# Seven block products instead of eight for the last batch's queries and keys, in a fused attention and FFN kernel

## The reference

```
q  = ln(x) @ W_q.T ;  kv = ln(x) @ W_kv.T           # 16 heads of 32
qf = fft(q) per head, divided by its norm ;  kvf likewise
kvf = cumsum(kvf over the rows of the batch)
x  = x + ifft(qf * kvf).real @ W_o.T
g  = silu((ln(x) @ fp8(gate_w)) * gate_scale) ;  u = (ln(x) @ fp8(up_w)) * up_scale
x  = x + ((g * u) @ fp8(down_w)) * down_scale       # inner width 1536
```

## Time and profile before

| what | value |
|---|---|
| time, median of 3 runs | 422.57 us (422.27 to 423.33) |
| profiled execution, span from first to last instruction | 419.2 us (the profile gives no other time for it) |
| TensorE busy | 411.5 us, 98% |
| VectorE busy | 281.3 us, 67% |
| ScalarE busy | 193.4 us, 46% |
| GpSimd busy | 102.5 us, 24% |
| granted TensorE clock, mean | 0.998 |

### The profile page before, as it was taken

One profiled execution on the slowest core, in us unless ns is written; L12 is line 12 of the kernel. 1 busy time (PEld: TensorE's weight loads), 2 busy tenths in 40 slices (PEclk: granted clock), 3 DMA queues, 4 the chain that ended last, 5 costly groups with the idle time before them and its releaser, 6 DMA issues.

```text
span 419.2 us, 5474 instructions
## 1 busy us (share of the span) xinstructions
PE 411.5 (98%) x1895; PEld 218.8 (52%) x1895; DVE 281.3 (67%) x497; ACT 193.4 (46%) x322; POOL 102.5 (24%) x108
## 2 busy tenths in 40 slices
PE   8999999999999999999999999999999999999994
PEld 4744454455455554554554564454555555555553
DVE  5999998999999694287676952186784744332234
ACT  3787656676755245546222573255342522122220
POOL 0133641015334322045350031043541001300003
PEclk9999999999999999999999999999999999999999
DMA  8986548600381144140112025320112041200002
GB/s 249 289 240 238 177 101 187 141 2 0 94 209 26 38 64 88 39 167 34 27 33 44 2 50 89 62 95 7 25 27 52 0 90 37 75 2 0 2 0 100
DMA packets 57546, 33.54 MB, mean 80 GB/s; under 512 B 49456, under 2 KB 49840, under 8 KB 57392
## 3 DMA queue, kind: packets, MB, share of 16 engines
q1 hardware_dynamic: 57088, 32.93, 30.7%
q10 hardware_dynamic: 432, 0.28, 0.2%
HBM read 17.44 MB, written 4.19 MB: 52 GB/s over the span
## 4 chain that ended last, share of the span: by engine, by line
PE 95%; DMA 1%; DVE 1%; SPq 1%; POOL 0%; POOLq 0%; issue 0%
PE bd L461 21%; PE bu L445 20%; PE bg L445 20%; PE ba L350 15%; PE ba L390 8%; PE bd L350 4%; PE ba L363 1%; DMA h<-x_dram 1%; PE bd L390 1%; PE bd L363 1%; PE bg L350 1%; PE bu L350 1%; PE bu L390 1%; PE bd L407 1%; PE bd L336 0%; PE bg L422 0%
## 5 line engine op out<-in xcount | busy, mean ns | idle before, releaser
L461 PE MATMUL bd<-dw,fu 128*128 128x512 f32 x376 | 100.0, 411 | 0.0
L445 PE MATMUL bu<-hT,gu 128*128 128x512 f16 x384 | 90.7, 379 | 0.0
L445 PE MATMUL bg<-hT,gu 128*128 128x512 f16 x376 | 89.2, 380 | 0.0
L461 PEld LDWEIGHTS bd<-dw,fu 128*128 128x128 f32 x376 | 70.6, 188 | 18.6 <-DVE fu L1165 0.7
L1160 DVE SCALAR_TENSOR_TENSOR ff<-bu,us,sl 128x512 f32<-128x512 f32 x48 | 35.9, 747 | 65.0 <-PE bu L445 61.8
L708 ACT ACTIVATE sl<-bg,gs 128x512 f32<-128x512 f32 x48 | 32.9, 686 | 80.2 <-PE bg L445 79.3
L350 PE MATMUL ba<-wf,xT 128*128 128x512 f16 x288 | 63.2, 379 | 0.0
L445 PEld LDWEIGHTS bu<-hT,gu 128*128 128x128 f16 x384 | 37.4, 98 | 45.6 <-DVE ff L1160 0.6
L445 PEld LDWEIGHTS bg<-hT,gu 128*128 128x128 f16 x376 | 34.1, 98 | 45.8 <-issue 8.9
L1165 DVE TENSOR_TENSOR fu<-ff,fu 128x512 fp32r<-128x512 f32 x47 | 40.1, 856 | 15.7 <-ACT fu L714 15.3
L1534 POOL TENSOR_TENSOR h<-ff,h 128x512 f32<-128x512 f32 x14 | 17.6, 1277 | 129.8 <-DVE ff L1186 129.8
(11 more groups left out here) (180 smaller groups left out, 449.9 us busy)
## 6 DMA issues: line engine op xcount, KB each, us to landing
h<-x_dram SPq DMA_DIRECT2D x16, 256.0 KB, 4.2
out_dram<-h SPq DMA_DIRECT2D x15, 256.0 KB, 2.0
hT<-w_q_dram SPq DMA_DIRECT2D x4, 256.0 KB, 3.8
gu<-w_kv_dram SPq DMA_DIRECT2D x4, 256.0 KB, 4.7
hT<-gate_w_dram SPq DMA_DIRECT2D x2, 512.0 KB, 3.8
hT<-up_w_dram SPq DMA_DIRECT2D x2, 512.0 KB, 5.9
gu<-woT_dram SPq DMA_DIRECT2D x1, 1024.0 KB, 5.5
hT<-down_w_dram SPq DMA_DIRECT2D x2, 512.0 KB, 5.0
```

The costliest lines, as they stand in the source:

```text
L445: m = e.matmul(bk[:, :], gu[:, c, 4 * w + k, col:col + P], hT[:, b % 2, part, k, :], start=k == 0 and part == 0, stop=k == KT - 1 and part ...
L461: m = e.matmul(bd[t][:, :], fu_at(n)[:, part, P * t:P * t + P], dw[:, i, :], start=i == 0 and part == 0, stop=i == NI - 1 and part == 1)
```

## The change

The rows of batch 3 are taken as two halves (tiles 0 and 1, tiles 2 and 3), the inner dimension as two halves (slices 0 and 1, slices 2 and 3) and the weights as queries and keys. The two by two blocks are multiplied with seven products instead of eight (Strassen's algorithm in Winograd's form). One product of one row pair j is 2 slices times 3 parts = 6 matmuls, 14 products in all.

- The four sums of weights (`dve_t`, 16 operations, in f32) are made on VectorE in batch 1's pass and split in high (`act_th`, 8) and low parts (`dve_tl`, 8).
- The rows of batch 3 are normalised pair by pair (`dve_x7`) and four sums of halves of them made (`dve_s7`, 256 columns each). Seven blocks of 256 columns per pair are rounded, split (`act_xh7`, `pool_xl7`) and transposed (`sp_x7`), where `xT` had four of 128 per tile.
- The products are added up in PSUM and by VectorE (`dve_u2`, `dve_u3`, `dve_c`, 10 operations); ScalarE copies two (`act_p1`, `act_first7`) and squares from SBUF (`act_sq7`). All 14 products stand ahead of batch 2's first gate/up step; none is left between the first two.
- The row statistics of batch 3 (`dve_stats1`, `dve_root0_head` and `_tail`) and its norm chain come earlier in VectorE's program. The constant that sets the scale of the folded weights is 2^-13 instead of 2^-14.

```diff
 tensor_program, pass b:
-                if nxt < NB:
+                if nxt < NB - 1:
                     pe_qk(e, nxt, 0, 0)
...
+                elif nxt < NB:
+                    for j in range(2):
+                        for p in SEVEN:                    # 1, 6, 2, 7, 5, 4, 3
+                            pe_seven(e, j, p)
                 pe_gate_up(e, b, 0)
                 pe_down(e, b * NI - 1)
-                if nxt < NB:
+                if nxt < NB - 1:
                     pe_qk(e, nxt, 3, 1)
 scalar_program, pass b:
                     act_qk(e, nxt, 1, 0)
+                    act_th(e, 0, 1)
                     act_qk(e, nxt, 1, 1)
+                    act_th(e, 0, 3)
                     act_qk(e, nxt, 2, 0)
+                    act_th(e, 0, 2)
+                    act_th(e, 0, 4)
+                    act_th(e, 1, 1)
+                    act_th(e, 1, 3)
+                    act_th(e, 1, 2)
+                elif nxt < NB:
+                    for j in range(2):
+                        act_p1(e, j)
+                        act_first7(e, j)
+                        act_sq7(e, j, 0)
...
                 act_silu(e, b * NI)
...
                 act_silu(e, b * NI + 3)
+                if b + 2 < NB:
+                    act_th(e, 1, 4)
 vector_program, pass b:
-                if nxt < NB:
+                if nxt < NB - 1:
                     dve_sum(e, nxt, 0, 0)
+                    dve_t(e, 0, 1)
                     dve_sum(e, nxt, 0, 1)
+                    dve_t(e, 0, 2)
+                    dve_t(e, 0, 3)
                     dve_sum(e, nxt, 1, 0)
+                    dve_t(e, 0, 4)
+                    dve_t(e, 0, 5)
                     dve_sum(e, nxt, 1, 1)
+                    dve_t(e, 0, 6)
+                    dve_t(e, 0, 7)
                     dve_sum(e, nxt, 2, 0)
+                    dve_t(e, 0, 8)
+                    dve_tl(e, 0, 1)
+                    dve_t(e, 1, 1)
+                    dve_tl(e, 0, 3)
+                    dve_t(e, 1, 2)
+                    dve_t(e, 1, 3)
+                    dve_tl(e, 0, 2)
+                    dve_t(e, 1, 4)
+                    dve_t(e, 1, 5)
+                    dve_t(e, 1, 6)
+                elif nxt < NB:
+                    for j in range(2):
+                        dve_u2(e, j)
+                        dve_u3(e, j)
+                        dve_sum(e, nxt, j, 0)
+                        dve_c(e, j, 5)
+                        dve_c(e, j, 4)
...
                 dve_scale_out(e, b - 1, 3)
-                if nxt < NB:
+                if nxt < NB - 1:
                     dve_sum(e, nxt, 3, 1)
+                elif nxt < NB:
+                    dve_norm_tail(e, nxt, range(NT))
+                    dve_scale(e, nxt, 0, 1)
                 dve_f(e, b * NI + 1)
...
                 dve_fu(e, b * NI + 1)
+                if b + 2 < NB:
+                    dve_tl(e, 0, 4)
+                    dve_t(e, 1, 7)
...
                     dve_product(e, nxt, 0)
+                if b + 2 < NB:
+                    dve_t(e, 1, 8)
+                    dve_tl(e, 1, 1)
+                    dve_tl(e, 1, 3)
                 dve_f(e, b * NI + 3)
...
                 dve_fu(e, b * NI + 3)
+                if b + 2 < NB:
+                    dve_tl(e, 1, 2)
+                    dve_tl(e, 1, 4)
+                    dve_stats1(e, b + 2, 1)
+                    dve_stats1(e, b + 2, 2)
                 if nxt < NB:
                     dve_zl(e, nxt, 1)
...
                     dve_o(e, nxt, 1)
+                if b + 2 < NB:
+                    dve_root0_tail(e, b + 2, range(NT))
+                    dve_x7(e, 0, 0)
+                    dve_x7(e, 0, 1)
+                    for n in (1, 2, 3, 4):
+                        dve_s7(e, 0, n)
```

More of the change, by code:

```diff
@@ L66, in tenancies @@
     for b in range(1, NB):
-        if b > 1:
-            order += [("qk", b, 0, w) for w in range(2)]
-        order += [("qk", b, t, w) for t in (1, 2, 3) for w in range(2)]
+        if b == NB - 1:
+            order += [("seven", j, p) for j in range(2) for p in SEVEN]
+        else:
+            if b > 1:
+                order += [("qk", b, 0, w) for w in range(2)]
+            order += [("qk", b, t, w) for t in (1, 2, 3) for w in range(2)]
         order += [("tri", b, 0)]
@@ L183, in build @@
         a_zh, v_zl = sem("act_zh"), sem("dve_zl")
+        s_seven, a_p1, a_xh7, p_xl7, a_th, v_tl = (
+            sem(n) for n in ("pe_seven", "act_p1", "act_xh7", "pool_xl7", "act_th", "dve_tl"))
+        v_t, v_x7, v_s7, v_u2, v_u3, v_c = (sem("dve_" + n) for n in ("t", "x7", "s7", "u2", "u3", "c"))
+        d_x7 = [sem(f"d_x7{n}") for n in range(3)]
         d_cst, d_cst2, d_id, d_wo, d_sc, d_carry = (sem("d_" + n) for n in ("cst", "cst2", "id", "wo", "sc", "carry"))
@@ L352, in pe_qk @@
             m.then_inc(s_qk, 1)
+        def pe_seven(e, j, p):
+            i, n = AT["seven", j, p], 7 * j + SEVEN.index(p)
+            held = {1: wf[:, 0, :, 0:2, :], 2: wf[:, 0, :, 2:4, :], 3: wf[:, 1, :, 2:4, :], 4: w_sum[4],
+                    5: w_sum[1], 6: w_sum[2], 7: w_sum[3]}[p]
+            vacant(e, ("seven", j, p))
+            e.wait_ge(d_x7[X_PIECE[p]], 32 * (j + 1))
+            if n == 1:
+                e.wait_ge(v_tl, 8)
+            first = p not in (2, 3)
+            for k in range(2):
+                for part_x, part_w in ((0, 0), (0, 1), (1, 0)):
+                    m = e.matmul(ba[i][:, :], xts[:, part_x, X_BLOCK[p] + k, P * j:P * j + P], held[:, part_w, k, :],
+                                 start=first and k == 0 and part_x == part_w, stop=k == 1 and part_x == 1,
+                                 skip_group_check=True)
+            m.then_inc(s_seven, 1)
         def pe_tri(e, b, t):
@@ L947, in scalar_program @@
                 act_silu(e, b * NI + 7)
+                if b + 2 < NB:
+                    act_root0(e, b + 2, range(NT))
+                    act_xh7(e, 0, 0)
+                    act_xh7(e, 0, 1)
+                    act_xh7(e, 0, 2)
                 if nxt < NB:
@@ L1587, in gpsimd_program @@
                 if b + 2 < NB:
[L1588 to L1591, removed]
+                    for j in range(2):
+                        for n in range(3):
+                            pool_xl7(e, j, n)
             pool_out(e, NB - 1, 0)
@@ L1606, in sp_xT, with sp_x7 @@
                 e.dma_start(xT[:, b % 2, part, :, P * t:P * t + P], xs[:, t % 2, part, :], transpose=True).then_inc(d_xT[t], 16)
+        def sp_x7(e, j, n):
+            lo, hi = X_COLS[n]
+            if j == 0 and n == 0:
+                e.wait_ge(s_qk, 8 * (NB - 1))
+            for part in range(2):
+                e.wait_ge((a_xh7, p_xl7)[part], 3 * j + n + 1)
+                e.dma_start(xts[:, part, lo // P:hi // P, P * j:P * j + P], xs7[:, part, lo:hi],
+                            transpose=True).then_inc(d_x7[n], 16)
         def sp_hT(e, b, t):
```

211 lines of the change are left out of this document (169 added, 42 removed).

## The result

The changed kernel takes 427.52 us (median of 6 runs, 426.48 to 429.62), the kernel before 422.42 in the same comparison (6 runs): ratio 1.0129, interval 1.0110 to 1.0148. It is 5.1 us slower. I had forecast 424.0 and a range to 426.3; slower was right, the size was not, and the time lies outside the range.

A forecast was written before the change was run, and what follows sets the result against it. TensorE was taken to bound the kernel, busy 411.47 of 419.20 us. The terms -2.60 + 1.15 + 1.6 + 0.6 + 0.1 + 0.6 = +1.45 us gave 424.0 us, range 420.9 to 426.3.

The forecast's parts named there:

- The saving: Twelve matmuls between batch 2's first two gate/up steps go: 2.60 us gained, the most the change can give.
- Step A: Start of batch 1's stretch: weight sums delay ScalarE's table load and first SiLU, TensorE waits for a bank; +1.15 us.
- Step B: Scan of batch 2: added VectorE operations and contention with GpSimd make tile 1's scan late; +1.6 us, bounds 0.3 to 3.5.
- Step C: Additions before zl(1): GpSimd's low part of ks for tile 3 late for its scan matmul; +0.6 us, bounds 0 to 1.2.
- The products of batch 3: The seven products per row pair run without stalls: 0 us, bounds 0 and 1.3.
- The transposes: 56 blocks instead of 32, 17.4 us of queue instead of 9.9, issued before they are needed: hidden.
- the rest of batch 1: Statistics and normalisations leave VectorE's queue later, where it is busy 11.67 of 18.00 us; +0.1 us, bounds 0 and 0.5.
- lower end of the sum: Saving with the lowest stalls: -2.60 + 0.3 + 0.3 = -2.0 us.
- Step D: FFN's start in batch 2: norm chain and a scale ahead of the second FFN product make it late; +0.6 us, 0.2 to 1.2.
- Rival 3: VectorE always goes first over GpSimd at the shared memory access, lengthening the scan's stalls: 426.4 us, chance 0.11.
- the first three: Rivals: additions absorbed, 421.1 us, chance 0.22; saving and stalls cancel, 422.4, 0.28; VectorE always first, 426.4, 0.11.
- rival 4: Matmul count stays or accumulating into a bank already read costs an interruption, no gain: about 426.6 us, chance 0.02.

The follow-up runs named there:

- run 5: Changed kernel with five late weight-sum operations moved from the scan of tiles 0 and 1 to behind the second attention output; 428.24 us, run once.
- run 1: Kernel before with only the 32 operations on weight sums added at the changed kernel's places, results unused; 426.16 us, ratio 1.0098.
- Run 3: Changed kernel with GpSimd's first low part of row pair 0 held back until VectorE's four half sums are done; 425.45 us, ratio 1.0078.
- no_sums: Changed kernel without the 32 weight-sum instructions, plain weight slices used in their place; 422.65 us, ratio 1.0014.
- late_sums2: late_sums with the norm chain between batch 2's scaled outputs and late fu parts ahead of the rows' normalisations; 420.97 us, ratio 0.9964 to the kernel before.
- Run 2: The same run as no_sums: changed kernel without the 32 weight-sum instructions; 422.65 us, 4.9 less than the changed kernel.
- late_sums: Changed kernel with roundings behind the first SiLU, GpSimd held back, norm chain behind the FFN product, seven weight-sum operations and pair 0's rows later; 422.38 us, ratio 1.0001.

## Why the prediction was wrong

**What held.** The bound was right: TensorE, where a late operand costs its lateness. The saving was 2.60 and nothing else shortened. Step A was right in its mechanism, and its wait by the bracket, 1.32 us, is 0.17 above the estimate (1.49 by the ledger, with the slower matmuls behind it); the last weight sum ended at 176.20 for 175.8 computed (the pass began 0.32 later). Step B was sized at 1.6 and is 1.85; its two parts, 0.85 by order and the rest by GpSimd, were found by run 5 as about 0.7 and 1.1. Step C was 0.6 and is 0.83, within its bounds, but not by the path that I named. The scan of tile 3 waits for nothing. The up step ahead of it waits 0.31 us: GpSimd's product of tile 1 ended late (two halves of 1.18 instead of 0.73, beside the low parts), and behind it ScalarE's copy, VectorE's `dve_zl`, its product of tile 2 and then the FFN product. The products of batch 3 cost nothing, as computed. The transposes stayed hidden: pair 1's were issued from 252.3 to 260.2, and its products begin at 267.6.

**The step that failed is "the rest of batch 1: +0.1 us", with bounds 0 and 0.5.** It measured 2.35 (1.27 and 0.50 in named waits; run 1 has 0.13 of it too, so the rows' halves cost 2.2). I had the rule in hand: in step B I priced a VectorE operation beside GpSimd's at 1.65 instead of 0.68. For the rows' half sums I took a mean instead, that VectorE is busy 11.67 of 18.00 us there, and held that idle time against the added operations. But this step brings its own GpSimd operations, 1.26 and 1.82 us long, started by the normalisation and ScalarE's rounding in the same step, and VectorE's third and fourth half sum meet them: they took 3.16 us in each of the six profiles that keep this order. Run 3 took nothing away but that meeting and got 2.1 us back, 2.2 by the trace. The operations that "leave the queue later" were true and of no use, since they were not in the way of the attention output. The range missed for the same reason: this term's upper end alone was 1.85 too low. With 2.35 in its place the sum is +3.7, and with A to D as measured +5.1. That this is the medians' difference to a tenth is partly luck, since the spans of the profiles differ by 5.5. (The lower end of the sum, -2.0, left out step D's own 0.2; it should read -1.8.)

**Step D was too small by half**, 0.6 for 1.19. The interval of 0.2 to 1.2 held it. The upper end was the case of a chain that waits for GpSimd's adds, and I took the middle. The chain did wait: its second operation took 0.95 us instead of 0.29 beside the last of GpSimd's three adds (they end at 288.02), as the timeline of VectorE shows.

```profile
286.24 0.94 DVE L1235 RECIPROCAL y<-Q 128x128 f32<-128x128 f32 x1
287.22 0.95 DVE L1237 SCALAR_TENSOR_TENSOR Q<-y 128x128 f32<-128x128 f32 x1
288.20 0.29 DVE L1239 TENSOR_TENSOR Q<-Q,S 128x128 f32<-128x128 f32 x1
```

In steps B and D I chose between a figure without GpSimd and one with it, and both times too near to the one without; in the rest of batch 1 I formed no figure with it at all. The rule of the Trainium skill that I set beside step B (GPSIMD Engine Reference, section 1 Specifications: VectorE and GpSimd share SBUF interfaces) bears on the failed step as well. Run 3 agrees with it there (3.16 us against 0.75), and so does run 5 in step B, whose 1.85 lies between the 1.6 taken and the 2.1 that I had computed for engines that alternate.

**Rival 3** (426.4) was nearest in time of the first three, but not in mechanism (rival 4, 426.6, is out: 12 matmuls are gone and the products have no gap): in step B the engines alternate, GpSimd's two operations being slowed by 0.38 and 0.45 us and VectorE's two low parts taking 1.22 each.

**What stays open.** The profiles differ by 2.6 us in when batch 1's pass begins (154.80 to 157.41 us), though up to there the kernels are the same but for semaphores, addresses and the constant of the folded weights. One part lies early: a row of 72 matmuls of `pe_qk` begins between 64.07 and 67.04 us (64.79 before, 64.07 in the changed kernel). The other is the wait for a SiLU near 99 us, the first line of the waits above: 1.00 us in the changed kernel, 1.00 in no_sums and 1.03 in late_sums2, 0.16 to 0.36 in six runs and none in three, the kernel before among them. In the changed kernel the SiLU stands behind a GpSimd add of one row, which took 1.80 us instead of 1.26, and beside it an operation of VectorE on the FFN's weights took 2.17 instead of 1.22. So this may be one more such meeting, settled by when the two happen to start. I didn't test it. Nor do the profiles say how often it happens in the other executions, so of the 5.1 us some tenths may come from there. Run 2's 4.9 against run 1's 3.9 has no explanation here: in the two passes the two profiles agree to 0.05 us.

## What to carry to other kernels

Here a saving on the engine that bounds the kernel was paid for on the engines that feed it, whose margins were 0.4 us in the scan: list for every added operation what stands behind it on its own queue, and when that is wanted. Before adding work to VectorE, look whether GpSimd works at that moment, and above all whether the added work itself starts GpSimd; idle time by a mean says nothing of it. Work that is needed by no one for long belongs behind the last operation with a small margin, and on ScalarE nothing that comes late should stand ahead of a table load that could run in idle time. The same operations in another order were 6.5 us apart.

## What the runs showed of the hardware

- **Who is held up.** Two 256-column sums of two SBUF tensors took 3.16 us beside two consecutive GpSimd operations of 1.26 and 1.82 us, and 0.75 without them. An FFN product, which reads one input from PSUM, took 0.74 beside GpSimd (199.16, with a GpSimd add of one row from 199.29 on) as elsewhere.
- **One SBUF input is not safe either.** In late_sums two normalisations (one SBUF tensor and two columns of scalars) took 2.79 us where two at 245.81 us took 0.99, beside GpSimd's 768-column low part:

```profile
241.53 2.79 DVE L1347 TENSOR_SCALAR qk<-h,mv,E 128x512 f32<-128x512 f32 x2
```
```profile
242.21 1.83 POOL L1786 TENSOR_TENSOR xw<-own,xw 128x768 f16<-128x768 f32 x1
```

- **A table load cost its own 1.28 us here.** In the changed kernel it starts 0.02 us behind the copy ahead of it (176.23 + 0.63), and the SiLU starts at 178.18, 1.30 behind the load's start. The Trainium skill, ScalarE: Activation LUTs, section What ACT_TABLE_LOAD costs, gives about 1283 ns for the load and about 1380 ns of drain beside it, 2.66 us in all. The first figure agrees; no second one shows at this place. With 2.66 for the load step A would have come to 2.5, an estimate by that page, and its wait is 1.3.
